# Masked cross-attention: a fourth group of row maxima at the head of each batch, eight units left in the loop over chunks

## The reference, cut to what matters

```python
q = query @ Wq + bq
kv = context @ Wkv + bkv          # k, v: (b, 16 heads, 1601, 16)
scores = jnp.einsum('bhid,bhjd->bhij', q, k) * scale
scores = jnp.where(mask[:, None, None, :], -jnp.inf, scores)
attn = jax.nn.softmax(scores, axis=-1)
out = jnp.einsum('bhij,bhjd->bhid', attn, v)
return out @ Wout + bout
```

## Time and profile before

| what | value |
|---|---|
| median of 3 runs | 2667.76 us (2666.96 to 2674.25) |
| profiled execution: own time | 2666.93 us |
| profiled execution: span | 2665.1 us |
| mean granted TensorE clock | 0.958 of full |
| PE / DVE / ACT / POOL busy | 2457.0 / 1432.5 / 975.5 / 583.1 us |
| first to last L820 (groups of the mask version) | 1197.7 to 1816.9 us, 180 matmuls, 45 groups |
| L675 in the mask version | 150 reductions, median 992 ns |
| L669 | 45 reductions, median 1830 ns |

### The profile page before, as it was taken

How to read it: one execution, slowest core, us unless ns; L and a number is a source line. 1 busy time by engine, 2 the same in 40 slices (tenths; PEclk the granted TensorE clock), 3 DMA queues, 4 the chain that set the end, 5 groups by cost and what they waited for, 6 DMA issues and landing times. The chain is left out here.

```text
span 2665.1 us, 91180 instructions
## 1 busy us (share of the span) xinstructions
PE 2457.0 (92%) x41601; PEld 1769.6 (66%) x41601; DVE 1432.5 (54%) x2340; ACT 975.5 (37%) x1286; POOL 583.1 (22%) x504
## 2 busy tenths in 40 slices
PE   7999999999998878979999999999879988998798
PEld 4776776776676655736676767676567777777466
DVE  4454454454453763365555454554556666666468
ACT  2333333333333331224444444443434433332223
POOL 2424433432441203231111111211011111111000
PEclk8999999999999659989999999999899999999899
DMA  2111111111010422121111111111100000000200
GB/s 96 33 39 33 33 39 33 28 38 39 27 39 9 182 82 65 56 80 33 45 34 45 40 39 39 39 39 47 55 2 4 4 3 3 4 3 4 83 1 16
DMA packets 56728, 102.30 MB, mean 38 GB/s; under 512 B 10272, under 2 KB 49024, under 8 KB 55024
## 3 DMA queue, kind: packets, MB, share of 16 engines
q1 hardware_dynamic: 54448, 91.35, 11.1%
q0 software_dynamic: 1904, 5.15, 0.5%
HBM read 90.30 MB, written 9.21 MB: 37 GB/s over the span
## 5 line engine op out<-in xcount | busy, mean ns | idle before, releaser
L675 DVE TENSOR_REDUCE x_mx<-banks 128x2 f32<-128x800 f32 (+1 forms) x422 | 416.5, 990 | 385.6 <-PE banks L843 268.1
L868 PE MATMUL banks<-x_wv,x_cT 128*128 128x256 f32 (+1 forms) x1664 | 421.3, 395 | 5.1 <-DVE x_nmb L685 5.1
L757 PE MATMUL banks<-x_cT,x_wk 128*128 128x400 f32 (+1 forms) x1024 | 381.8, 515 | 7.2 <-DMA x_cT<-in_ctx 5.7
L868 PEld LDWEIGHTS banks<-x_wv,x_cT 128*128 128x128 f32 (+1 forms) x1664 | 297.8, 188 | 70.1 <-issue 11.0
L556 ACT ACTIVATE x_PT<-banks 128x2048 f32<-128x2048 f32 (+1 forms) x112 | 196.6, 1755 | 357.9 <-PE banks L905 357.9
L558 ACT ACTIVATE x_PT<-banks,x_kbs 128x1024 f32<-128x1024 f32 (+1 forms) x208 | 221.1, 1110 | 233.1 <-PE banks L905 233.1
L757 PEld LDWEIGHTS banks<-x_cT,x_wk 128*128 128x128 f32 x1024 | 187.9, 192 | 137.5 <-issue 23.3
L905 PE MATMUL banks<-x_qbd,x_kT 32*128 32x128 f32 x6656 | 246.9, 273 | 0.0
L905 PEld LDWEIGHTS banks<-x_qbd,x_kT 32*128 32x128 f32 x6656 | 242.6, 183 | 3.6
L432 POOL TENSOR_TENSOR x_kbf<-x_kT,x_mb 128x400 bf16<-128x400 f32 (+1 forms) x128 | 122.7, 961 | 556.8 <-ACT x_kT L490 556.6
L885 PE MATMUL banks<-x_PT,x_V 128*32 128x64 f32 x13312 | 233.3, 221 | 1.1 <-ACT x_PT L556 0.3
(11 more groups left out here) (406 smaller groups left out, 3696.2 us busy)
## 6 DMA issues: line engine op xcount, KB each, us to landing
x_cT<-in_ctx SPq DMA_DIRECT2D x96, 400.0 KB, 3.7
x_cT<-in_ctx SPq DMA_DIRECT2D x32, 401.0 KB, 3.7
e_up<-in_mo_up SPq DMA_DIRECT2D x9, 512.0 KB, 15.6
e_down<-in_mo_down SPq DMA_DIRECT2D x9, 512.0 KB, 16.4
x_mrow<-in_mask_row SPq DMA_DIRECT2D x1, 3202.0 KB, 14.3
t_w<-in_db_w SPq DMA_DIRECT2D x3, 1024.0 KB, 8.4
e_rows<-in_c_unfilled SPq DMA_DIRECT2D x1, 2967.0 KB, 13.1
e_xg<-e_rows SPq DMA_DIRECT2D x23, 129.0 KB, 2.0
```

Of the source, the lines that this page charges most:

```text
L675: dve.reduce_max(mx[:, H0[k]:H0[k] + 3:2, kb], g.PS[:, first:first + 2, 0:KBS[kb]], AXX).then_inc(max_read, 1)
L757: last = pe.matmul(PJ[pb][:, 0:KBS[k]], wk[:, c, gg, :], cT[:, (p + 1) % 2, c, KB0[k]:KB0[k] + KBS[k]], start=c == 0, stop=c == KC - 1)
L868: last = pe.matmul(PJ[pb][0:CHK[c + k], D * k:D * k + D], cT[:, p, cc, 128 * (c + k):128 * (c + k) + CHK[c + k]], wv[:, cc, :], start=cc = ...
```

## The change

The pair (key block 1, group 1) goes from the loop to the head as a fourth group. On TensorE it stands behind the keys of block 3, ahead of the output projection and the values of chunk 0; on VectorE behind group 2, ahead of the addition of the output. The loop keeps eight units, with other slots: none behind the scores of pair 2, one behind its attended values, none behind its projected values, and one less at pair 10.

```diff
--- before.py
+++ after.py
@@ -337,15 +337,15 @@
         VALUED = {2: 2, 4: 5, 6: 8, 8: 11, 10: 14}
         PROJECTED = {0: 0, 2: 3, 4: 6, 6: 9, 8: 12, 10: 15}
         H0 = [0, 1, 4, 5]
-        HEADED = [(0, 0), (0, 1), (1, 0)] if mask else []
+        HEADED = [(0, 0), (0, 1), (1, 0), (1, 1)] if mask else []
         NHD = len(HEADED)
         KP = 2 if mask else 1
         ALL = [(kb, k) for kb in range(NKB) for k in range(4)]
         LOOPED = [(kb, k) for kb, k in ALL if (kb, k % 2) not in HEADED]
         if mask:
-            SCORED = {2: 1, 4: 3, 6: 5, 8: 7, 10: 9}
-            PROJECTED = {0: 0, 2: 2, 4: 4, 6: 6, 8: 8}
-            VALUED = {}
+            SCORED = {4: 2, 6: 4, 8: 6}
+            VALUED = {2: 1}
+            PROJECTED = {0: 0, 4: 3, 6: 5, 8: 7}
 
         def units(batches):
 
@@ -675,7 +675,7 @@
                     dve.reduce_max(mx[:, H0[k]:H0[k] + 3:2, kb], g.PS[:, first:first + 2, 0:KBS[kb]], AXX).then_inc(max_read, 1)
 
                 ahead_of = NHD if ahead and attend else 0
-                for j in range(ahead_of - 1):
+                for j in range(2 if ahead_of else 0):
                     headed(j)
                 if tail and attend:
                     denominators()
@@ -684,8 +684,8 @@
                     dve.wait_ge(full[pb], bank.value(pb, use))
                     dve.tensor_tensor(nmb[:, :, :], PJ[pb][:, None, 0:128].to_broadcast([128, NPR, 128]),
                                       pmask[:, :, None].to_broadcast([128, NPR, 128]), ALU.mult).then_inc(free[pb], 1)
-                if ahead_of:
-                    headed(NHD - 1)
+                for j in range(2, ahead_of):
+                    headed(j)
                 if plan.WO and attend:
                     add_output()
 
@@ -949,6 +949,8 @@
                         headed(2)
                     if ahead and b:
                         key_block(bank, plan, i, p, NKB - 1)
+                    if ahead and NHD:
+                        headed(3)
                     if plan.WO:
                         output()
                     project_values(0)
```

## The result

The changed kernel takes 2672.46 us (median of 20 runs, 2665.57 to 2681.68), the kernel before, run beside it, 2665.81 (20 runs). One of these, 3093.82, was in a slow state and is not in the ratio. The ratio of the runs is 1.0027, interval 1.0017 to 1.0037: slower by 0.27%, or 7.2 us (4.5 to 9.9). Forecast were +6.6 us and 2673.5, with 0.63 for "the same", within some 8 us, and 0.33 for slower. The profiled execution took 2675.70 us, its span 2673.9, 8.8 more than before. A single execution isn't fine enough for such a difference; 2.1 us of the 8.8 lie ahead of the first group at all. So I compare piece by piece.

A forecast was written before the change was run, and what follows sets the result against it. TensorE bounds the kernel, busy 2457.0 of 2665.1 us. Even batches +1.5, odd +2.8 (both with the loop's -0.15 a batch) and batch 0 +2.3 make +6.6 on 2666.93: 2673.5 us, range 2668.5 to 2678.

The forecast's parts named there:

- Even heads: Head of the 7 even batches: fourth group ahead of the output projection, its reduction hidden; +0.36 us each.
- Odd heads: Head of the 7 odd batches: the scores must wait for the fourth group's reduction; +0.55 us each.
- Batch 0: First batch, once: the third group's whole reduction shows as a wait; 2.46 us at the head, +2.3 with the loop.
- the dearer case: First batch: half clock lasts through the scores of chunk 0, so the head's 2.46 us grows to 3.7 or 3.8.
- Pair 2: Loop, unit moved behind the attended values: 4.51 us instead of 4.36 between scores, +0.15 a batch.
- The unknown entry into a unit from attended values: Loop, the moved unit's new slot: entering it costs between nothing and 0.09 us; 0.05 taken.
- Pair 4: Loop, unit ahead of the scores gone: scores 0.15 us shorter and 0.15 less wait for VectorE, -0.30 a batch.
- Pair 6: Loop: keeps two units, so nothing changes.
- Pair 10: Loop, unit behind the scores gone: the 0.3 us becomes waiting for the exponentials, so no gain.
- The rival that it comes free: Rival (C), loop's end: the removed unit saves 0.3 us in 15 batches, 4.5; +2.1 in all, 2669.0; chance 0.19.
- Rival (B): Head of the first batch: half clock to the end of the scores, 3.8 us; 8.5 slower, 2675.4; chance 0.22.
- (D): Whole kernel faster by over 8 us, needing 0.7 us from each of 15 batches after paying the group; chance 0.04.

The follow-up runs named there:

- the last experiment: The changed kernel, but in batch 0 the values of chunk 0 stand between the third and the fourth group; ratio 1.0034 to the kernel before.

## Why the prediction was right

- **The order of sizes held: head, batch 0, little from the loop.** Forecast +6.6 us; the runs say 7.2 (4.5 to 9.9). That the absolute time came within 1.0 us of 2673.5 has some luck in it: the base of the sum, 2666.93, lay 1.1 above the median of the later runs, the growth 0.6 below the measured one.
- **Even heads: 0.36 forecast, 0.48 measured.** The step took the group's entry and itself, and left the work behind it unchanged. The output projection behind a group takes 1.83 to the values, not 1.72, the 0.11 that was missing. The values show a like tenth: 1.82 to L897 behind the output projection, 1.92 between attended values and a unit, where both neighbours are tiled. The group brings two switches between row-tiled and full matmuls, and I had counted one.
- **Odd heads: 0.55 forecast, 0.65 measured.** The wait for the reduction was there, with L897 2.37 and not 2.28 behind the group. The reduction started and ended as forecast (0.40 and 1.82); TensorE followed after 0.15 where I had taken 0.05; why is told below, at pair 6.
- **Batch 0: +2.3 forecast for the whole batch (2.46 at the head, less 0.15 in the loop), +2.79 measured.** The wait is 2.46 as forecast; the half clock adds 0.37 at the scores and 0.08 at the values, and the loop gives 0.13 back. It was the dearer case that I had kept as an upper bound of 3.8, not the whole of it. I had taken the clock to rise as long after the last hole as before. It rose 3.9 us behind the third group before (it is at 0.57 from 1206.2 to 1206.6) and 5.0 behind the fourth after (at 0.76 from 1212.0 to 1212.3).
- **Pair 2: +0.15 forecast, +0.08 measured.** The unknown entry into a unit from attended values costs nothing more; of 0 to 0.09 I had taken 0.05. The other 0.02 was a misreading: the 1.94 from the values to L897 in the earlier trace rows held a unit, which starts at 1434.77, 0.02 ahead of L897. Without it the way is 1.92.
- **Pair 4: -0.30 forecast, -0.30 measured**, and shown apart by leaving a unit out.
- **Pair 6: nothing forecast, +0.09 measured.** This step failed. Its two units are further apart: in the changed kernel 1.53 from one L843 to the next, before 1.44 (1434.77 to 1436.21 at pair 4). The timeline of TensorE and VectorE there:

```profile
1446.39 0.34 PE L843 MATMUL banks<-x_kbf,x_qbf 32*128 32x400 bf16 x2
...
1446.78 0.99 DVE L675 TENSOR_REDUCE x_mx<-banks 128x2 f32<-128x800 f32 x1 [2.24 <-PE banks L843]
...
1447.92 0.34 PE L843 MATMUL banks<-x_kbf,x_qbf 32*128 32x400 bf16 x2
```

  The reduction ends at 1447.77, as soon as ever, and the second unit starts 0.15 later; before, at pair 4, 0.06 after the end at 1436.15. What differs is the unit's number. Units are counted through the key blocks, and the first unit of a block also waits for that block's keys (`kbf_done`). Before, the loop's later blocks begin with units 2 and 6, which stand behind projected values and come 1.8 us after the reduction. In the change the block begins with unit 4, just the one that must wait. Its keys are long there (GpSimd's last copy of them ended at 1433.35), but the wait for the reduction now is an instruction of its own ahead of the weight load (L839 in queue PEldq, 51 ns; 14 of them from batch 1 on), and the weight load starts 0.12 instead of 0.05 behind the reduction's end. The first line is from before, the others are from the change:

```profile
1436.20 0.10 PEld L843 LDWEIGHTS banks<-x_kbf,x_qbf 32*128 32x128 bf16 x2 [0.17 <-DVE x_mx L675]
1447.89 0.12 PEld L843 LDWEIGHTS banks<-x_kbf,x_qbf 32*128 32x128 bf16 x2 [0.24 <-issue]
L839 PEldq EVENT_SEMAPHORE x1: 51/51/51, 1447.8 to 1447.8; - x1
```

  Two of the experiments compare the two forms in one slot, behind the scores of pair 2 with a unit ahead of them. With three groups (one unit moved to pair 0) unit 2 begins a block there, and the pair takes 4.44; with four (units spread) it doesn't, and the pair takes 4.35. The reduction and the unit behind it, in the first of them, then in the second:

```profile
1428.28 0.99 DVE L675 TENSOR_REDUCE x_mx<-banks 128x2 f32<-128x800 f32 x1 [1.20 <-PE banks L843]
...
1429.42 0.34 PE L843 MATMUL banks<-x_kbf,x_qbf 32*128 32x400 bf16 x2
```
```profile
1429.59 0.99 DVE L675 TENSOR_REDUCE x_mx<-banks 128x2 f32<-128x800 f32 x1 [1.21 <-PE banks L843]
...
1430.64 0.34 PE L843 MATMUL banks<-x_kbf,x_qbf 32*128 32x400 bf16 x2
```

  From the reduction's end that is 0.15 and 0.06. No run adds a second wait and nothing else, but all eight traces follow the rule. The tenth at pair 8 when a unit at pair 4 is left out is the same: there unit 6 begins a block. So is that of the odd heads: L897 waits for the reductions, the exponentials and the spread maxima at once.
- **Pair 10: nothing forecast, nothing measured**, with the unit gone from either kernel. The rival that it comes free has fallen.
- **The errors partly cancel:** even +0.12, odd +0.10, pair 6 +0.09, pair 2 -0.07, pair 10 -0.02 a batch, +0.45 in batch 0 for the half clock, together 2 us, which is what lies between 6.6 and the 8.6 of the pieces.

Rival (B), the half clock, was true in its mechanism and a third of its size (0.45 of 1.3). (D) needed more than a batch could give: even leaving a unit out gave 0.3 at best.

Open: what the delays of single batches are, and whether four groups would pay with batch 0 left at three; no kernel here tried that. The tenth of a switch between tilings is read from rows that agree; no run varied it by itself.

## What to carry to other kernels

Two pieces of the same work are worth different times by slot: on the bounding engine a unit cost 0.30 where it stood beside another, and nothing where that engine waits for a third one anyway. Before moving work to save it, look for the slots in which the bounding engine waits, and fill them first: moving one unit there gained 4 us, bundling two units into a group lost 7. See also which piece falls into a slot where it must wait: one that has a second condition to wait for, though long met, started 0.09 later than one that hasn't. And count the neighbours: a block put between two others also changes the time of the block behind it, and the first pass of a loop, where the usual cover is missing, pays a wait in full.

## What was unexpected of the hardware

- A block of full matmuls behind a row-tiled group takes 0.11 us longer to the next block than behind full ones (L860: 1.83 against 1.72), besides the 0.09 at the group's entry. "Mode switching requires drain" (the Trainium skill, "TensorEngine Tiling (Array Packing)", "Key Properties") agrees; the traces give the price, about a tenth of a microsecond at either side.
- A unit that waits for VectorE's reduction alone starts 0.06 us behind its end; one that also waits for a semaphore met long ago starts 0.15 behind it, in each of 14 batches. The compiled program then has the wait for the reduction as an instruction ahead of the weight load.
- A hole of 2 us on TensorE just after the clock had risen was followed by half clock, 0.51 over 3.5 us of full work (the last experiment). Whether that costs anything is decided by the slot behind the hole: the 1.3 us by which it lengthened the values of pair 0 fell into a wait and were hidden, the 0.32 at the scores ahead of them were not.
